# A new start for a single-core attention and mixture-of-experts kernel: x loaded as a whole ahead of the weights, projection weights from ScalarE's queue, biases put in place by their own transfers, and a new order of steps

## What is computed

```
q = x@wq + bq;  k = x@wk + bk;  v = x@wv + bv            # q, k: 8 wide, v: 64 wide
x1 = gamma * softmax(q k^T) v + x                        # per image, 256 x 256 scores
s  = layernorm(x1)
r  = sum over 8 heads of tril(s Q_h s^T) (s E_h^T)       # causal, no softmax
x2 = x1 + r
s2 = layernorm(x2)
d  = top-2 of softmax(s2@gate_w + gate_b), renormalised  # 16 experts
out = x2 + sum_e d_e * ((silu(s2@w1_e) * (s2@w2_e)) @ w3_e)
```

## Time and profile before

| | |
|---|---|
| median of the timed runs | 108.12 us (107.54 to 109.13) |
| the profiled execution | 106.93 us, span 105.2 us, mean granted clock 0.993 |
| TensorE matmuls | 94.7 us busy (90% of the span), 620 instructions |
| VectorE | 69.5 us (66%), 208 |
| ScalarE | 51.7 us (49%), 105 |
| GpSimd | 43.0 us (41%), 57 |
| chain that ended last | TensorE 85%, VectorE 5%, issue 3%, DMA 2%, ScalarE 2% |

### The profile page before, as it was taken

How to read it: one execution, slowest core, us unless ns; L and a number is a source line. 1 busy time by engine, 2 the same in 40 slices (tenths; PEclk the granted TensorE clock), 3 DMA queues, 4 the chain that set the end, 5 groups by cost and what they waited for, 6 DMA issues and landing times.

```text
span 105.2 us, 1920 instructions
## 1 busy us (share of the span) xinstructions
PE 94.7 (90%) x620; PEld 52.7 (50%) x620; DVE 69.5 (66%) x208; ACT 51.7 (49%) x105; POOL 43.0 (41%) x57
## 2 busy tenths in 40 slices
PE   0248999999999999898999999999999999999990
PEld 0045977876697777675633632332333243324290
DVE  0455997997245684393477699999593999088061
ACT  4106998174454374406495559634361657062220
POOL 5874002211002040000033997292937696959300
PEclk9999999999999999999999999999999999999997
DMA  1278993000000000000039996000099991001002
GB/s 25 14 154 200 193 187 59 3 6 0 0 0 0 6 3 0 0 6 0 7 117 357 428 424 274 6 3 0 16 268 411 421 433 69 0 0 29 21 0 50
DMA packets 9516, 11.02 MB, mean 105 GB/s; under 512 B 6019, under 2 KB 8211, under 8 KB 8739
## 3 DMA queue, kind: packets, MB, share of 16 engines
q1 hardware_dynamic: 9410, 10.86, 33.3%
q0 software_dynamic: 96, 0.04, 0.7%
HBM read 10.57 MB, written 0.33 MB: 104 GB/s over the span
## 4 chain that ended last, share of the span: by engine, by line
PE 85%; DVE 5%; issue 3%; DMA 2%; ACT 2%; DVEq 0%; ACTq 0%
PE bank L868 27%; PE bank L882 13%; PE bank L684 6%; PE bank L799 5%; PE bank L769 4%; PE bank L786 4%; PE bank L826 4%; PE bank L811 4%; PE bank L743 3%; PE bank L731 2%; DMA x_in<-in_x 2%; PE bank L916 2%; PE bank L756 2%; PE bank L678 1%; PE bank L843 1%
## 5 line engine op out<-in xcount | busy, mean ns | idle before, releaser
L387 POOL TENSOR_TENSOR hid<-uu,dbc 128x512 f32<-128x512 f32 x24 | 30.7, 1306 | 11.9 <-DVE uu L642 9.3
L868 PE MATMUL bank<-s2T,w_in 64*128 64x512 f32 x128 | 32.0, 620 | 0.3 <-DVE uu L642 0.2
L476 ACT ACTIVATE sil<-bank 128x512 f32<-128x512 f32 x32 | 19.1, 598 | 18.6 <-PE bank L868 18.5
L377 POOL TENSOR_TENSOR rstd<-veps,neg_half 128x2 f32<-128x2 f32 x8 | 5.6, 697 | 40.8 <-DVE veps L504 40.8
L868 PEld LDWEIGHTS bank<-s2T,w_in 64*128 64x128 f32 x128 | 10.7, 185 | 17.3 <-ACT sil L476 10.0
L642 DVE TENSOR_TENSOR uu<-bank,sil 128x512 f32<-128x512 f32 x24 | 16.1, 686 | 1.8 <-ACT sil L476 1.5
L882 PE MATMUL bank<-hid,w_in 128*64 128x512 f32 x60 | 14.4, 604 | 0.0
L648 DVE TENSOR_TENSOR uu<-bank,dbc 128x512 f32<-128x512 f32 x8 | 5.5, 688 | 9.0 <-PE bank L868 7.7
L656 DVE TENSOR_TENSOR hid<-uu,sil 128x512 f32<-128x512 f32 (+1 forms) x9 | 8.5, 954 | 0.3
L882 PEld LDWEIGHTS bank<-hid,w_in 128*64 128x64 f32 x60 | 3.7, 136 | 9.3 <-issue 8.0
L591 DVE TENSOR_TENSOR omega<-bank,tri 128x512 f32<-128x512 f32 x8 | 5.2, 686 | 4.5 <-PE bank L786 4.5
(11 more groups left out here) (118 smaller groups left out, 132.5 us busy)
## 6 DMA issues: line engine op xcount, KB each, us to landing
dbc<-dispatch_scratch SPq DMA_DIRECT2D x6, 1024.0 KB, 9.2
dbc<-dispatch_scratch SPq DMA_DIRECT2D x4, 512.0 KB, 4.5
w_in<-in_L_ffn_w SPq DMA_DIRECT2D x3, 512.0 KB, 7.8
out<-x SPq DMA_DIRECT2D x4, 64.0 KB, 1.7
x_in<-in_x SPq DMA_DIRECT2D x1, 192.0 KB, 4.1
q_in<-in_L_attn_Q SPq DMA_DIRECT2D x2, 64.0 KB, 3.5
e_in<-in_L_attn_E SPq DMA_DIRECT2D x1, 128.0 KB, 3.5
x_in<-in_x SPq DMA_DIRECT2D x1, 64.0 KB, 2.0
```

The source lines that it names most:

```text
L387: nc.gpsimd.tensor_tensor(hid[:, i % HID], uu[:, i % UU], dbc[:, e, :], ALU.mult).then_inc(hid_done, 1)
L476: nc.scalar.activation(sil[:, i % SIL], banks[U1_BANK[i % 2]][:], ACT.Silu).then_inc(sil_done, 1)
L868: nc.tensor.matmul(banks[bank[i % len(bank)]][:], w_in[rows, HIDDEN * e:HIDDEN * (e + 1)], s2T[rows, half * HALF:(half + 1) * HALF], start ...
```

## The change

SyncE issues the rest of x right behind image 0 of x. wq, wk and wv are issued by ScalarE, ahead of its first activation, with the same shapes. bq and bk are no longer loaded into a staging tile and copied by VectorE: their transfers write the four copies into the zeroed row themselves, after a wait for the first memset, which is now that of the row; TensorE's "bias" waits for these transfers. The step "bias row" is gone. Behind this the list of steps and the table of banks are new. The start of the new list and the loads:

```diff
-    [("transpose x", 0), ("stack x", 0), ("stack x lo", 0), ("split wqk", 0), ("bias row", 0), ("bias", 0),
-     ("project qk", 0), ("bias col", 0), ("qk hi", 0), ("transpose x", 1), ("transpose x", 2), ("qk lo", 0),
-     ("stack x", 1), ("score", 0), ("stack x", 2), ("transpose x", 3), ("stack x lo", 1), ("project v", 0),
...
+    [("transpose x", 0), ("stack x", 0), ("bias", 0), ("transpose x", 1), ("stack x", 1), ("split wqk", 0),
+     ("transpose x", 2), ("stack x lo", 0), ("bias col", 0), ("stack x", 2), ("project qk", 0), ("stack x lo", 1),
+     ("qk hi", 0), ("stack x lo", 2), ("project qk", 1), ("project qk", 2), ("qk hi", 1), ("transpose x", 3),
+     ("qk lo", 0), ("score", 0), ("qk lo", 1), ("qk hi", 2), ("project v", 0), ("transpose e", 0), ("project v", 1),
+     ("score", 1), ("max", 0), ("stack x", 3), ("exp", 0), ("transpose prob", 0), ("qk lo", 2), ("copy prob", 0),
+     ("score", 2), ("copy v", 0), ("max", 1), ("exp", 1), ("stack x lo", 3), ("project v", 2), ("max", 2),
+     ("attend", 0), ("exp", 2), ("copy v", 1), ("transpose prob", 1), ("residual 1", 0), ("rstd 1", 0),
+     ("copy v", 2), ("project qk", 3), ("copy prob", 1), ("transpose prob", 2), ("attend", 1), ("copy e", 0),
+     ("normalise 1", 0), ("copy prob", 2), ("qk hi", 3), ("attend", 2), ("transpose s", 0), ("gram", 0),
+     ("residual 1", 1), ("stack s", 0), ("query", 0), ("rstd 1", 1), ("qk lo", 3), ("score", 3), ("project v", 3),
+     ("copy gram", 0), ("copy query", 0), ("normalise 1", 1), ("transpose s", 1), ("max", 3), ("stack s", 1),
+     ("residual 1", 2), ("gram", 1), ("query", 1), ("exp", 3), ("copy query", 1), ("copy v", 3), ("rstd 1", 2),
+     ("causal", 0), ("mask", 0), ("transpose prob", 3), ("carry", 0), ("causal", 1), ("copy prob", 3),
+     ("copy gram", 1), ("within", 0), ("mask", 1), ("carry", 1), ("copy y", 0), ("normalise 1", 2),
...
+     ("weigh", 6), ("silu", 12), ("weigh", 8), ("times", 10), ("down", 3), ("times", 11), ("weigh", 9),
+     ("times", 12), ("down", 4), ("transpose weights", 1), ("weigh", 10), ("up", 13), ("copy weights", 1),
+     ("silu", 13), ("up", 14), ("times", 13), ("silu", 14), ("up", 15), ("weigh", 12), ("times", 14), ("up", 16),
+     ("silu", 15), ("times", 15), ("up", 17), ("weigh", 13), ("silu", 16), ("times", 16), ("up", 18), ("down", 5),
+     ("silu", 17), ("silu", 18), ("down", 6), ("weigh", 14), ("down", 7), ("spread weights", 1), ("times", 17),
...
@@ SyncE @@
             sp.dma_start(x_in[:, 0:TILES, :], x_tok[:, 0:TILES, :]).then_inc(ld_x0, 16)
-            for m, w in enumerate((wq, wk)):
-                sp.dma_start(wqk_in[:, m, :], w.unsqueeze(0).to_broadcast([2, C, QK])).then_inc(ld_wqk, 16)
+            sp.dma_start(x_in[:, TILES:NT, :], x_tok[:, TILES:NT, :]).then_inc(ld_x, 16)
+            sp.wait_ge(zeroed, 1)
             for m, b in enumerate((bq, bk)):
-                sp.dma_start(b_in[0:1, m, :], b.unsqueeze(0)).then_inc(ld_b, 16)
-            sp.dma_start(wv_in[:], wv.unsqueeze(0).to_broadcast([2, C, C])).then_inc(ld_wv, 16)
-            sp.dma_start(x_in[:, TILES:NT, :], x_tok[:, TILES:NT, :]).then_inc(ld_x, 16)
+                sp.dma_start(b_row[0:1, m, :, 0:QK],
+                             b.unsqueeze(0).unsqueeze(0).to_broadcast([1, 4, QK])).then_inc(ld_b, 16)
@@ GpSimd @@
+            pool.memset(b_row[:], 0.0).then_inc(zeroed, 1)
             pool.memset(ident[:], 0.0).then_inc(zeroed, 1)
-            pool.memset(b_row[:], 0.0).then_inc(zeroed, 1)
@@ ScalarE @@
+            for m, w in enumerate((wq, wk)):
+                act.dma_start(wqk_in[:, m, :], w.unsqueeze(0).to_broadcast([2, C, QK])).then_inc(ld_wqk, 16)
+            act.dma_start(wv_in[:], wv.unsqueeze(0).to_broadcast([2, C, C])).then_inc(ld_wv, 16)
@@ VectorE @@
-                if name == "bias row":
-
-                    dve.wait_ge(ld_b, 32)
-                    nc.vector.tensor_copy(b_row[0:1, :, :, 0:QK],
-                                          b_in[0:1].unsqueeze(2).to_broadcast([1, 2, 4, QK])).then_inc(b_row_ready, 1)
@@ TensorE, step "bias" @@
-                    pe.wait_ge(b_row_ready, 1)
+                    pe.wait_ge(ld_b, 32)
```

More of the change, by code:

```diff
@@ L107 @@
 U1_BANK, U2_BANK, Y_BANK, OUT_BANK = (0, 1), (2, 3, 4), (5, 6), (7, 5)
 BANKS = (
-    0, 1, 2, 3, 4, 5, 6, 7, 0, 1, 2, 3, 4, 5, 7, 6, 0, 3, 1, 2, 5, 3, 7, 1, 5, 3, 1, 4, 7, 5, 3, 4, 6, 0, 7, 5,
-    1, 3, 6, 0, 2, 1, 7, 5, 3, 4, 2, 1, 7, 6, 0, 4, 5, 3, 2, 1, 7, 6, 4, 0, 5, 3, 2, 1, 7, 4, 0, 6, 5, 2, 3, 1,
-    7, 6, 7, 6, 7, 6)
+    0, 1, 2, 3, 4, 5, 6, 7, 0, 1, 2, 3, 4, 5, 6, 7, 3, 0, 1, 4, 2, 3, 7, 6, 0, 4, 2, 5, 1, 6, 0, 2, 3, 7, 5, 1,
+    6, 3, 4, 0, 2, 5, 1, 6, 4, 3, 7, 5, 1, 0, 2, 3, 7, 6, 4, 5, 1, 0, 2, 3, 7, 4, 6, 3, 5, 1, 6, 0, 2, 5, 3, 1,
@@ L112 @@
+    6, 7, 6, 7, 6, 7)
 USES = {"bias": ["bias"], "transpose x": ["xT"], "project qk": ["q", "k"], "transpose e": ["eT"], "project v": ["v"],
@@ L158, in hybrid_kernel @@
         wqk_in = sb("wqk_in", [P, 2, QK])
-        b_in = sb("b_in", [1, 2, QK])
         b_row = sb("b_row", [1, 2, 4, 32])
@@ L229, in hybrid_kernel @@
         zeroed, consts = sem("zeroed"), sem("consts")
-        b_row_ready, wqk_ready, wv_ready = sem("b_row_ready"), sem("wqk_ready"), sem("wv_ready")
+        wqk_ready, wv_ready = sem("wqk_ready"), sem("wv_ready")
         tri_ready, gram_zeroed = sem("tri_ready"), sem("gram_zeroed")
```

27 lines of the change are left out of this document (added).

## The result

The changed kernel takes **104.23 us** (median of 4 runs, 103.62 to 104.53) against 107.83 of the kernel before (107.48 to 109.13): ratio 0.967, 95% interval 0.960 to 0.974. A second batch gave 104.27 and again 0.967.

What follows compares the result with a forecast made beforehand. TensorE was taken as the bound from 9.5 us on, so an earlier start moves its dense stream forward: 1.9 + 0.1 = 2.0 us off the 108.12 median gives 106.1 us, with 8 in 10 between 104.8 and 108.3.

Steps and rivals of the forecast that it cites:

- lead: How far TensorE's dense stream moves forward: 2.35 us at attend 0, 1.9 at transpose s 0, kept to the end.
- What bounds the kernel: TensorE, busy 91.53 of 93.20 us from 9.5 us on; a changed start is worth what it moves that stream forward.
- Biases ... I take 4.7.: Bias transfers issued behind x land at 4.7 us, within 4.4 to 6.5, replacing VectorE's 1.30 us copy.
- The start: TensorE's first steps: biases at 4.75 us, project qk 0 at 5.95 against 6.93, score 0 at 8.95 against 9.46.
- Nothing of the new order lengthens TensorE's work, so the lead stays.: From transpose s 0 to the end: same matmuls in slightly other order, so the 1.9 us gained stays.
- I work out a difference on the profiled span and take it off the median.: Method: gain worked out on the profiled execution (106.93 us, span 105.2), then subtracted from the timed median of 108.12.
- The clock: TensorE's upper clock level from about 10 us; at 12, up to 0.5 us more (106.6); earlier, about 105.6.
- More than the lead: Rival, 18%: the order also removes waits of 0.5, 0.4 and 0.2 us and brings the clock level earlier; 105.3 us.
- The transfers only change places: Rival, 12%: shared DMA engines delay the biases to 6.5 us and project qk 0 to 7.75; lead 0.3, 107.8 us.
- Weights late: Rival, 17%: ScalarE's table load precedes its DMA issues, wk lands at 5.4 to 5.8 us; lead 0.8, 107.3 us.
- slower: Rival, 10%: six "up" (13 to 18) without a "down" between overload VectorE and make TensorE wait; 109.1 us.
- signs named for being wrong: Table load first on ScalarE, casts over 0.5 us, biases after x, or TensorE waits over 0.3 between 20 and 100 us.

Runs made afterwards that it cites:

- new_early: Changed kernel with its first 87 steps in the new order and the rest in the old order: 105.98 us, ratio 0.986 to the kernel before.
- new_late: Changed kernel with its first 87 steps in the old order and the rest in the new order: 106.62 us, ratio 0.992 to the kernel before.
- before_fill: Kernel before plus identity matmuls in TensorE's idle time, seven behind image 0's transposes, one behind image 2's: 106.95 us against 108.44, ratio 0.986.
- gamma_late: Changed kernel with GpSimd's transfers of gamma and bv issued behind the gate's bias: 104.03 us, ratio 0.967 to the kernel before.
- after_again: Changed kernel, unedited, run and profiled a second time: 104.27 us, ratio 0.967 to the kernel before.
- after: Changed kernel in its first batch and profile: 104.23 us, ratio 0.967 to the kernel before.

## Why the prediction was wrong

The time came out 1.9 us below the forecast (104.2 and 106.1). 1.2 of them are the profiled execution of the kernel before, which stood that far below the median of 108.12 from which the forecast was taken off; 0.3 are that of the changed kernel, which stood that far above its own median; 0.4 are the difference of the two profiles, 2.4 us where 2.0 were forecast. Those 2.4 are themselves two errors that partly cancel, which is luck: less lead from the start, and more behind it.

- *What bounds the kernel, and that the load order, the lost bias copy and the new queue matter through TensorE's stream.* Right. Weights on ScalarE are worth about 1.2 us with the new order, the table load is behind the issues as assumed, wk landed by 4.5 (4.2 forecast).
- *"Biases ... I take 4.7."* Wrong: 6.18. It was within the bounds (4.4 to 6.5), but I chose by size ("they are tiny and resemble x0 more"), and the size decided nothing: wv's rows on the same engines did. I had seen that wq and wk ran on two engines and used it only for a rival. Putting the biases in place by transfer therefore freed 0.4 us, not 1.8, and project qk 0 came 0.3 later than before, where I had it 1.0 earlier.
- *The start.* Score 0 was forecast at 8.95 and came at 10.04; attend 0 12.7 and 13.6; lead at transpose s 0 1.9 and 1.54. The later the step, the smaller the error: the work done ahead (qk 1, qk 2, image 3) counted as forecast.
- *"Nothing of the new order lengthens TensorE's work, so the lead stays."* This step failed. The lead grew by 1.2 us between transpose s 0 and the first "up". I had the two waits in the earlier trace rows and gave their removal 18%, half price; I had walked the new order only to "within" 0. Walking it to the two waiting steps would have shown that each has more work ahead of it now (between "query" 3 and "causal" 3 TensorE also has "transpose s2" 0 and 1, "carry" 2 and "gram" 3). The two waits are 0.9 of the 1.2 us, and new_early and new_late show that the order behind the first 87 steps carries this part. Behind the first "up" 0.35 us were lost again by the slow "hid", which the prediction didn't have.
- *"I work out a difference on the profiled span and take it off the median."* This step failed too, and cost more: 1.2 us. The profiled execution stood 1.2 below the median, and I took that as scatter. It had the clock's level rise at 11.7; the second profile, 108.22 and so within 0.1 of the median, has it at 14.5 and is 1.17 us later at transpose s 0. The change brings the rise to 9.9 to 11.5, so the gain against the usual execution is larger. In *The clock* I had costed its moment by 0.5 us either way from a single profile; before_fill shows 1.5 us for the old order. Of the two profiles of the changed kernel the first, 0.3 us longer, has the slow "hid" (0.8 us) and the earlier rise (0.5).
- *The rivals.* "More than the lead" was the right mechanism, at a larger size than allowed. "The transfers only change places" named the shared engines and the biases at up to 6.5, and priced it at a lead of 0.3; the biases were nearly that late (6.18) and the lead was 1.5. Project qk 0 came 1.2 us behind the forecast, and 0.3 of that was made up by attend 0 and 0.5 more by transpose s 0, where the rival had 0.2 in all. "Weights late" and "slower" did not happen: no wait among "up" 13 to 18, VectorE less loaded. Of the signs named for being wrong one did come: TensorE waits 0.5 and 0.8 us at 53 and 59 us.
- Summed on the second profiles: 106.5 - 102.5 = 4.0, of which 2.22 before transpose s 0, 1.21 up to the first "up", 0.58 in the experts' part. The first profiles had 1.54, 1.21 and -0.35. So of the 1.6 us between the two sums 0.7 lie before transpose s 0 (1.17 by the level in the kernel before, less 0.5 in the changed one) and 0.9 in the experts' part, where only the first profile of the changed kernel has the slow "hid".

What stays open: why the level rises where it does. Six matmuls more did not bring it forward (13.8), seven did (5.7) and so did eleven (8.5), each seen in one profile only; the median of before_fill is the evidence that it holds for most executions. Open too is how often "hid" and "weigh" meet in timed executions, and so how much of the differences under 1 us between variants is theirs.

## What to carry to other kernels

Compare the profiled execution with the median before subtracting anything from it: where it lies a per cent off, look for what differs between executions (here TensorE's clock level in the first 15 us), since a change of the start changes that too. List the bound engine's waits over the whole span and follow each in a new order, not only those near the edit. And a small transfer that everyone waits for is as late as whatever shares its DMA engines, so see how many engines each neighbour uses, and let the waiting engine do the work that doesn't need it first. Where two engines reach for the same moment (here "hid" and "weigh"), one profile shows one outcome: take a second one before a difference of under 1 us is put down to the change.

## What the runs showed of the hardware

- The same kernel is 1.17 us apart at 20 us, and about 1.3 in the span, with the moment at which TensorE's matmuls go from 0.41 to 0.28 us (11.7 or 14.5 us). The granted clock of the profile reads 1.00 on both sides of it; the trace's clock records begin there.
- A cast pair takes 0.33 or 1.38 us and a 64-element copy 0.18 or 1.30, depending on which of them meets GpSimd's DMA issue and memset. A subtraction of two SBUF tiles beside the same memset is not slowed (0.29 us, gamma_late).
- VectorE's product of two SBUF tiles takes 0.75 or 1.70 us and GpSimd's "weigh" 1.73 or 1.27, by which of the two starts first (after_again and after); TensorE then waits 0 or 0.8 us.
- A 16 KB weight read twice, issued by another engine 0.1 us before the second bias, delays it by 1.0 us (6.18 against 5.20): two of its four 32-byte pieces start as the weight's last packets end (5.39 and 5.53 against at most 4.55).
